# Queries' third part as a difference on GpSimd, and the rows of ones and the logits' weight products made first

## The reference

```python
x = x + tanh(g_xattn[0]) * xattn(layernorm(x), ctx, ctx, Wq, bq, Wk, bk, Wv, bv, Wo, bo)
x = x + tanh(g_ffn[0]) * ffn(layernorm(x), Wg, W1, b1, W2, b2)
...
# xattn: x is 32 x 112 x 256, ctx is 32 x 375 x 128, 16 heads of 16
scores = einsum('bhqd,bhkd->bhqk', qh, kh) / sqrt(16);  out = softmax(scores) @ vh @ Wo + bo
# ffn: 3584 tokens, 8 experts; each expert takes its best 896 tokens
S = sigmoid(tokens @ Wg).T;  G, I = top_k(S, 896)
out = (gelu(tokens[I] @ W1 + b1) @ W2 + b2) * G
```

## Time and profile before

| | us |
|---|---|
| median of three runs | 879.79 |
| lowest and highest | 879.17, 880.84 |
| profiled execution: its own time | 878.82 |
| profiled execution: span of the trace | 876.8 |
| TensorE busy | 792.2 (90%) |
| VectorE, ScalarE, GpSimd busy | 647.3, 566.3, 409.8 |

### The profile page before, as it was taken

How to read it: one execution, slowest core, us unless ns; L and a number is a source line. 1 busy time by engine, 2 the same in 40 slices (tenths; PEclk the granted TensorE clock), 3 DMA queues, 4 the chain that set the end, 5 groups by cost and what they waited for, 6 DMA issues and landing times. The chain is left out here.

```text
span 876.8 us, 22206 instructions
## 1 busy us (share of the span) xinstructions
PE 792.2 (90%) x8304; PEld 652.9 (74%) x8304; DVE 647.3 (74%) x1600; ACT 566.3 (65%) x1196; POOL 409.8 (47%) x531
## 2 busy tenths in 40 slices
PE   5889999999999999999993029999999999999995
PEld 3544788888888888888872017989898888888895
DVE  6767888888888889888853876787676766765542
ACT  2545878888887888887772125656657584839470
POOL 4554145544445544455434502565556564744504
PEclk9999999999999999999997559999999999999998
DMA  8661677777776777776412104162535444352303
GB/s 181 163 145 37 134 172 174 171 168 177 179 179 172 168 170 186 172 182 162 118 46 68 51 4 146 49 148 52 138 61 129 99 92 129 74 136 57 43 1 42
DMA packets 96482, 104.62 MB, mean 119 GB/s; under 512 B 12016, under 2 KB 92544, under 8 KB 96384
## 3 DMA queue, kind: packets, MB, share of 16 engines
q1 hardware_dynamic: 84128, 88.50, 40.1%
q0 software_dynamic: 10752, 14.69, 9.7%
q10 hardware_dynamic: 1504, 0.12, 0.2%
HBM read 39.60 MB, written 14.68 MB: 62 GB/s over the span
## 5 line engine op out<-in xcount | busy, mean ns | idle before, releaser
L505 DVE TENSOR_REDUCE a_nm<-a_pS 112x1 f32<-112x375 f32 x350 | 181.4, 540 | 35.6 <-PE a_pS L881 30.9
L1849 PE MATMUL e_p<-w2hl,e_hh 128*128 128x512 f32 x440 | 156.9, 397 | 0.0
L872 PEld LDWEIGHTS a_pT<-a_qst,a_kst 98*128 98x128 bf16 x1536 | 112.9, 98 | 38.1 <-issue 6.5
L1643 POOL DMA_INDIRECT out_dram<-e_y,e_idx x56 | 89.1, 1592 | 110.7 <-ACT e_y L1682 100.0
L872 PE MATMUL a_pT<-a_qst,a_kst 98*128 98x112 bf16 x1536 | 138.0, 212 | 1.7 <-ACT a_room L322 1.1
L718 POOL TENSOR_TENSOR a_kp<-a_k_rest,a_kp 128x375 bf16<-128x375 f32 x56 | 50.7, 908 | 170.3 <-ACT a_kp L342 170.3
L1851 PE MATMUL e_p<-w2hl,e_hl 128*128 128x256 f32 x440 | 122.9, 279 | 0.0
L881 PE MATMUL a_pS<-a_kst,a_qst 96*112 96x375 bf16 x350 | 111.9, 329 | 1.9 <-DVE a_nm L505 1.7
L1729 DVE TENSOR_TENSOR e_hl<-e_hid,e_hh 128x384 fp32r<-128x384 f32 (+1 forms) x128 | 77.8, 623 | 47.2 <-ACT e_hh L1675 46.4
L322 ACT ACTIVATE a_P<-a_pT 128x448 f32<-128x448 f32 x192 | 97.0, 541 | 23.8 <-PE a_pT L872 23.6
L322 ACT ACTIVATE a_room<-a_pT 128x448 f32<-128x448 f32 x192 | 100.0, 539 | 10.4 <-PE a_pT L872 10.3
(11 more groups left out here) (277 smaller groups left out, 1683.7 us busy)
## 6 DMA issues: line engine op xcount, KB each, us to landing
a_kst<-a_kp SPq DMA_DIRECT2D x192, 192.0 KB, 3.5
w<-in_L_ffn_W_dram SPq DMA_DIRECT2D x16, 1024.0 KB, 6.6
a_qst<-a_qp SPq DMA_DIRECT2D x96, 112.0 KB, 3.4
a_craw<-in_ctx_dram SPq DMA_DIRECT2D x32, 128.0 KB
a_room<-in_x_dram SPq DMA_DIRECT2D x8, 448.0 KB, 5.1
a_xb<-in_x_dram SPq DMA_DIRECT2D x32, 112.0 KB, 3.0
out_dram<-a_x SPq DMA_DIRECT2D x32, 112.0 KB, 2.0
xn_scratch<-a_x SPq DMA_DIRECT2D x32, 112.0 KB, 2.2
```

Source lines behind the costliest of these rows:

```text
L505: dve.tensor_reduce(nm[:, h:h + 1], s_bank(b, h)[0:LQ, 0:LK], AXX, ALU.max, negate=True).then_inc(s_used, 1)
L872: last = pe.matmul(pT[u % 2][:, j * LQ:(j + 1) * LQ], kst[b % 4][:, h, c * 128:(c + 1) * 128], q_of(b, slice(None), h), start=True, stop=True)
L1643: pool.indirect_dma_start(out=out, out_offset=bass.IndirectOffsetOnAxis(ap=idx[r % 2][:, g:g + 1], axis=0), in_=y[g][:], in_offset=None, c ...
L1849: pe.matmul(p2[g % 2][:], hh[:, f, rows], T.w2hl[r % 2][:, f].rearrange("p q d -> p (q d)"), start=(f == 0), stop=(f == 7), skip_group_che ...
```

## The change

- **Queries.** ScalarE writes the high part, VectorE writes queries + bias - high part to SBUF in fp32 (`q_remainder`, one instruction for each half, into `q_rest`, a piece of `P[1]`). ScalarE writes the middle part from there, and GpSimd subtracts it to get the low part (`q_low_part`). The 32 residual matmuls go. A bank of queries is free once `q_remainder` has read it.
- **Order on VectorE.** `q_remainder(j, 0)` stands ahead of `x_copies`, `q_remainder(j, 1)` behind it, both ahead of the maximum number 5. The old `q_low` pair stood behind it and behind number 7.
- **Rows of ones.** All four memsets (L692) move in front of GpSimd's first normalisation. `q_low_part` of round g - 2 follows the normalisation for round g.
- **Weights of the logits.** The mean and the transposes stand ahead of the first `x_transposes`, the product of `Wo` and the centred `Wg` right behind it, and the bias's part joins the product for `bo` in round 0. VectorE's two copies stand in front of and behind the second group's statistics. `Wg` and `Wo` are loaded ahead of `Wq`, and the first `x_scale` still stands behind the scaling of `Wq`.
- In the main loop and in `experts` only waits are changed: GpSimd's logits wait for a later VectorE instruction, ScalarE waits for the copied gates.

```diff
@@ loads, on SyncE
             x_group(0)
+            sp.wait_ge(mean_set, 1)
+            sp.dma_start(wg[:, :, 0:NE], ...).then_inc(wg_loaded, 16)
+            sp.dma_start(wo[:, :, 0:D], ...).then_inc(wo_loaded, 16)
             sp.dma_start(wq_raw[:], ...).then_inc(wq_loaded, 16)
             x_group(1)
-            sp.wait_ge(wg_padded, 1)
-            sp.dma_start(wg[:, :, 0:NE], ...).then_inc(wg_loaded, 16)
...
@@ ScalarE, one round
-                q_piece(j, 0, 0)
+                q_high_part(j, 0)
...
-                q_piece(j, 0, 1)
-                if j == 2:
-                    act.wait_ge(wot_ready, 1)
-                    act.activation(woT.rearrange("p k n -> p (k n)"), pS[1][:], ACT.Copy).then_inc(wot_copied, 1)
+                q_high_part(j, 1)
                 x_logits_copy(j)
-                q_piece(j, 1, 0)
+                q_mid_part(j, 0)
...
-                q_piece(j, 1, 1)
+                q_mid_part(j, 1)
@@ VectorE
-            def q_low(g, t):
-                dve.wait_ge(q_ready[t], 3 * g + 3)
-                dve.tensor_scalar(q_part(2, g, t), by_pair(pQ[t]), bq[:, t:t + 1], None, ALU.add).then_inc(q_cut[t], 1)
+            def q_remainder(g, t):
+                dve.wait_ge(q_high[t], g + 1)
+                wait(dve, q_low[t], g)
+                dve.scalar_tensor_tensor(by_pair(q_rest[t]), by_pair(pQ[t]), bq[:, t:t + 1], q_part(0, g, t),
+                                         ALU.add, ALU.subtract).then_inc(q_read[t], 1)
...
                 maxima(2, 5)
+                q_remainder(j, 0)
                 if j + 1 < DVE_COPIES:
                     x_copies(dve, j + 1)
+                q_remainder(j, 1)
                 maxima(5, 6)
-                q_low(j, 0)
...
-                q_low(j, 1)
@@ GpSimd
+            for i in range(4):
+                ones(i)
             for g in range(1, G):
                 x_norm(g)
-                if g >= 4:
-                    ones(g - 4, g)
+                for t in range(2):
+                    if g >= 2:
+                        q_low_part(g - 2, t)
@@ TensorE, one round
-                q_rest(j, 1, 0)
...
-                q_rest(j, 1, 1)
                 x_logits_back(j)
                 early_s(5, 6)
-                q_rest(j, 2, 0)
...
-                q_rest(j, 2, 1)
-                gate_part(j)
```

More of the change, by code:

```diff
@@ L714, in _ @@
                     pool.memset(V[g - 1][:, :, :, DK:DK + 1], 1.0).then_inc(v_set, 1)
+            for g in (G - 2, G - 1):
+                for t in range(2):
+                    q_low_part(g, t)
             def k_low_part(b, t):
@@ L784, in q_product @@
             def q_product(g, t):
[L785 removed]
+                wait(pe, q_read[t], g)
                 for k in range(2):
@@ L970, in _ @@
             pe.wait_ge(ident_set, 3)
-            x_transposes(0)
+            pe.wait_ge(mean_set, 2)
+            pe.wait_ge(wg_loaded, 16)
+            for k in range(2):
+                last = pe.matmul(pS[1][:, 256:256 + NE], mean_of, wg[:, k, 0:NE], start=(k == 0), stop=(k == 1))
+            last.then_inc(gate_made, 1)
+            pe.wait_ge(wo_loaded, 16)
+            for k in range(2):
+                for r in range(2):
+                    last = pe.transpose(pS[0][:, r * D + k * 128:r * D + (k + 1) * 128], wo[:, k, r * 128:(r + 1) * 128],
+                                        T.ident[:])
+            last.then_inc(gate_made, 1)
+            x_transposes(0)
+            pe.wait_ge(gate_kept, 1)
+            pe.wait_ge(wot_copied, 1)
+            for k in range(2):
+                for r in range(2):
+                    last = pe.matmul(pS[1][:, 256 + k * NE:256 + (k + 1) * NE], woT[:, r, k * 128:(k + 1) * 128], wgc[:, r, :],
+                                     start=(r == 0), stop=(r == 1))
+            last.then_inc(gate_made, 1)
             pe.wait_ge(wq_ready, 2)
@@ L1023, in _ @@
                 if j == 0:
[L1024 to L1025 removed]
+                    pe.wait_ge(bv_ready, 2)
                     for k in range(2):
[L1027 removed]
+                        pe.matmul(pK[0:LQ, 0:DX], bv_wide[:, k, :], wo[:, k, :], start=(k == 0), stop=False, skip_group_check=True)
+                    for k in range(2):
+                        last = pe.matmul(pK[0:LQ, D:DX], bo_wide[:, k, :], wgc[:, k, :], start=False, stop=(k == 1), skip_group_check=True)
                     last.then_inc(bo_ready, 1)
                 early_s(6, 8)
[L1030 to L1031 removed]
             for m in range(FIRST, LAST):
```

123 lines of the change are left out of this document (45 added, 78 removed).

## The result

The changed kernel takes **883.38 us** in the median of 8 runs (882.2 to 884.7), the kernel before 879.6 in 8 runs: ratio 1.0048, with a 95% interval of 1.0036 to 1.006. It is slower by 0.5%; I had forecast 877.6 and a range of 872.5 to 882. The profiled execution took 882.2 (span 880.5), 3.4 more than that of before.

The account below looks back on a forecast made before the run. The main loop's order is unaffected, so the time depends on when the opening lets it begin. Rounds 1 to 4 -5.8, start +3.3, rounds 5 to 7 +0.3: -2.2 from a median of 879.8 gives 877.6 us, range 872.5 to 882.

Parts of the forecast that it names:

- The lock: VectorE's SBUF-to-SBUF copies and scalings wait for a GpSimd memset's end; inferred from two rows, 0.21 us lost in each.
- Rival A: At the start, memsets cost little, 1.3 us at most, or VectorE isn't held: 874.8 us, chance 0.20.
- The start: Before round 1: four early memsets hold VectorE, so round 1 begins at 24.65 instead of 21.33 us, +3.3 us.
- scaling `Wq` and the root bring the four L494 to 10 us: At the start, these VectorE steps let the four L494 come at 10 us instead of 8.17.
- rival C: Memsets slip between VectorE's instructions, 2.65 us each: one slip gives 880.2, two give 882.9 us; chance 0.13.
- Rounds 1 to 4: Opening rounds: 7.8 us a round, longer in rounds 1 and 2, sum 34.0 against 39.84 us, -5.8 us.
- Rounds 5 to 7: End of the opening: residuals go but remainders stand ahead of maximum 5; 10.75, 8.0 and 8.3 us, +0.3 us.
- What the opening gains or loses reaches the end of the program one for one: Main loop: its order depends on nothing the change makes, so only its beginning, 87.94 us before, matters.
- Rival D: Round 5's low clock stays for one more round, costing some 5 us: 882.6 us, chance 0.07.
- `experts` taken at 0: In `experts`, added waits cost 0 us, since ScalarE idles there before its scalings.

Follow-up runs that it names:

- after_again: The changed kernel without an edit, traced and measured a second time: 885.3 us, ratio 1.0061 to the kernel before.
- ones_early_only: The kernel before with only the four memsets of the rows of ones moved to GpSimd's front: 885.0 us, ratio 1.0054.
- clock_kept: The changed kernel with filler matmuls, never read, in round 7 (10) and ahead of the attention's last two products (8): 880.7 us, ratio 1.0012.
- before_gaps: The kernel before with filler matmuls ahead of round 5 (7) and ahead of the attention's last two products (8): 877.4 us, ratio 0.9972.
- all_together: The changed kernel with fillers in TensorE's pauses, `V` fills at GpSimd's front, reordered loads, memsets in rounds 6, 7 and the main loop: 873.3 us, ratio 0.9946.
- ones_in_gaps: The changed kernel with two memsets moved to round 6, one to round 7, one to the main loop, no fillers: 878.0 us, ratio 1.0000.
- ones_late: The changed kernel with the four memsets back in rounds 3 to 6, behind GpSimd's normalisations: 881.8 us, ratio 1.0029.
- split_gaps: The changed kernel with one memset at GpSimd's front, three behind the opening, and fillers in TensorE's pauses: 876.8 us, ratio 0.9960.

## Right and wrong, step by step

- **The lock: right.** Taken from two short overlaps of 0.21 us, it held in full: L477, L591, L502 (in after_again) and a cast all waited for a memset's end. Rival A is out.
- **The start: mis-sized, +3.3 forecast, +5.5 measured.** The failed step is "scaling `Wq` and the root bring the four L494 to 10 us": I let the third memset run beside the scaling and made only L494 wait for it. The scaling is SBUF-to-SBUF itself, and it is two instructions, so it waited twice, 5.23 us for 0.66. What should have run beside the third and fourth memset (the root, four L494, the second statistics) came behind the last one, and GpSimd's first normalisation began at 20.11 instead of 17.35. The first of the two slips is that of rival C, in the very place where it had been put ("between L469 and the scaling of `Wq`"), with a chance of 0.13 for the rival. Its argument against itself, that GpSimd stood back behind VectorE's row of L494, doesn't hold for memsets: the last memset slipped in between two scalings that follow each other without a pause, and in ones_early_only, where `Wq` isn't late and VectorE doesn't pause, a memset begins between the scalings too. That rival C's 882.9 lies next to the measured 883.4 is luck: it had two more waits of 2.65 at the start, which grew by only 2.2 over the forecast, and the rest came from behind the opening.
- **A slip in the sum.** 7.96 less 0.7 plus 0.4 is 7.66, not 7.3: the start should have read +3.7 and the whole -1.8. The stretch from the first normalisation to round 1 then took 6.74.
- **Rounds 1 to 4: right in the sum, in part by luck** (-6.2, forecast -5.8; 33.68 and 34.0). One by one they took 8.33, 7.96, 7.62 and 9.77, where 9.3, 8.7, 7.8 and 8.25 were forecast, so that too long a first half made up for too short a fourth round. In after_again they took 36.35. The range was too narrow: there round 1 was 1.1 us longer, with a short instruction of VectorE on the other side of one of GpSimd, and rounds 2 to 4, with the clock low once more, 1.6.
- **Rounds 5 to 7: +0.5, forecast +0.3.** The wait of 1.27 for maximum 5 came in round 7 as named. What I left out is that the clock fell behind it.
- **"What the opening gains or loses reaches the end of the program one for one": wrong.** This is the second failed step: the sentence stood at the head and was never tested against the clock. The lag grew by 1.0 at the main loop's first iteration and by 1.0 at the attention's last product. clock_kept shows both to be the granted clock. Rival D had the mechanism, at 5 us and in other rounds. In before_gaps and all_together, with fillers in TensorE's pauses, the lead at the main loop's beginning does reach 450 us (-1.87 and -1.86, -4.85 and -5.00).
- **The last expert: +1.5, unforeseen.** With `experts` taken at 0 I had only looked at the added wait. That wait isn't the cause: all_together and ones_in_gaps have it and take 40.72, and ones_early_only doesn't have it and takes 41.30.

With the start at +5.5 and the rest of my sum the profiled execution would have taken the 878.8 of before, no change. It took 882.2. The rest are the clock (2.0), the last expert (1.5), routing (0.3) and the rounds (-0.4 and +0.2), together 3.6, which is the difference of the spans; by the executions' own times it is 3.4. The median of the changed kernel lies another 1.2 above its profiled execution.

**What stays open.** ScalarE's pause in the last expert is 1.8 to 2.2 us in six traces, 0.7 to 0.8 in five, and absent in before, before_gaps, ones_in_gaps and all_together. In the changed kernel TensorE's matmuls run on beside it for 2.0 of its 2.1 us, so it is hardly the products that are late. One packet of the queue that loads instructions moves in these microseconds (25.9 us into the expert; the pause ends at 26.7), but in ones_late one moves at 25.9 too, when its pause of 0.7 is already over (25.3), and in ones_in_gaps at 25.9 with no pause. So 1.5 of the 3.6 us have a place but no cause. Open too are what else decides the clock's falls, and how far the steps of the rounds, each from one trace, would come again.

## What to carry to other kernels

A GpSimd instruction over few partitions isn't cheap for others: look at what VectorE runs beside it from SBUF to SBUF, count each scaling or cast of VectorE there as one wait of up to the GpSimd instruction's length, and put the memset where VectorE has none, which can be a gap of a few microseconds in the middle of the program. Where TensorE pauses again and again, ask of each change which pause it makes longer and what stands at the low clock behind it; a few matmuls that nobody reads are a cheap test. And where short instructions of two engines race for the same moment, look at two traces of a kernel before believing either. Give the kernel before the same help (here the fillers) before crediting a gain to the change.

## What the runs showed of the hardware

- VectorE's TENSOR_SCALAR, and its CAST, from SBUF to SBUF waited for the end of a GpSimd memset of two partitions: 1.52 for 0.17, 5.23 for 0.66 (two), 1.94 for 0.17. BATCH_NORM_STATS2 (0.41 in the changed kernel, at 5.90), the maxima, which read PSUM (0.55 in split_gaps, at 90.15), and instructions with two tensors in SBUF (0.16 to 0.18) weren't held by one. Beside a GpSimd instruction that reads SBUF the latter took 0.55 and 0.97 instead of 0.16. The Trainium skill, "SBUF — State Buffer", section "SBUF: two separate sides", makes this distinction: instructions with two SBUF inputs are held only by a GpSimd instruction that reads SBUF. The traces agree here too.
- Two GpSimd memsets back to back don't keep VectorE out, nor two scalings GpSimd: they took turns, one instruction each, in the changed kernel (8.31 to 13.86) and in ones_early_only.
- The granted clock fell to 1.2 GHz behind pauses of which the longest was 1.27 us (changed kernel, 85 to 87.3 us: TensorE busy 0.42 and 0.12 in two whole microseconds), and it was low until 90.7 although TensorE was busy from 88 on. In clock_kept, busy 1.00 and 0.64 in two such microseconds, it didn't fall. In all_together it fell at 456.3 behind four microseconds with 0.70 to 0.80 busy and no pause above 0.30, and in the kernel before, with the same four, it stayed at 2.4 GHz.
